# Scores from keys that are carried through the folded matrix, eight batches at a time, in place of projected queries

## The reference, cut to what matters

```python
vcq = concatenate([v, where(row_zero, 0, q)], -1)
self_feat = vcq @ W_self.T + b_self
output = self_feat
for d in range(2):
    A = adj if d == 0 else swapaxes(adj, 1, 2)
    A = A[:, :, :20, :]
    cond, vb = A.sum(-1), A @ w_bias + b_bias
    kv = self_feat[:, :20]
    qh, kh = heads(self_feat @ Wq[d].T + bq[d]), heads(kv @ Wk[d].T + bk[d])
    aff = einsum('bnhd,bmhd->bnhm', qh, kh) / sqrt(32)
    w = softmax(where(cond > 0, aff, -9e15) + vb)
    output += einsum('bnhf,hgf->bnhg', einsum('bnhm,bmf->bnhf', w, kv), Wout[d]) + bout[d]
return v + relu(output)
```

## Time and profile before

| what | value |
|---|---|
| median of 3 runs | 1905.44 us |
| the profiled execution's own time | 1906.23 us |
| its span | 1904.4 us |
| TensorE matmul busy | 1887.3 us (99%), 11020 records |
| VectorE busy | 1303.7 us (68%) |
| ScalarE busy | 575.5 us (30%) |
| GpSimd busy | 836.6 us (44%) |
| granted TensorE clock | 0.999 of full |

### The profile page before, as it was taken

The page is one execution under the profiler, slowest core; times in us unless marked ns, Lnnn a source line. Parts: engine busy times, 40 slices in busy tenths (PEclk is TensorE's granted clock), DMA queues, the critical chain, the costliest instruction groups (busy, mean ns, idle before and its releaser), DMA issues.

```text
span 1904.4 us, 34516 instructions
## 1 busy us (share of the span) xinstructions
PE 1887.3 (99%) x11020; PEld 1646.9 (86%) x11020; DVE 1303.7 (68%) x1897; ACT 575.5 (30%) x1189; POOL 836.6 (44%) x746
## 2 busy tenths in 40 slices
PE   8999999999999999999999999999999999999999
PEld 6899999888888888888888888888888888888887
DVE  3433232477777777777777777777777777777776
ACT  3333232233333333333333333333333333333332
POOL 0332222354444444444444444444444444444443
PEclk9999999999999999999999999999999999999999
DMA  7123324544444444444444444444444444444431
GB/s 214 34 84 89 96 90 99 136 113 122 122 122 119 118 120 121 121 121 121 121 121 121 121 121 121 121 121 121 121 121 121 121 121 121 121 121 121 121 100 63
DMA packets 227951, 219.87 MB, mean 115 GB/s; under 512 B 58176, under 2 KB 179008, under 8 KB 223808
## 3 DMA queue, kind: packets, MB, share of 16 engines
q1 hardware_dynamic: 223440, 219.24, 42.6%
q10 hardware_dynamic: 4464, 0.02, 0.1%
HBM read 164.39 MB, written 54.79 MB: 115 GB/s over the span
## 4 chain that ended last, share of the span: by engine, by line
PE 95%; DVE 1%; DMA 0%; issue 0%; SPq 0%; POOL 0%; ACT 0%; ACTq 0%; DVEq 0%
PE bank L1517 37%; PE bank L1463 19%; PE bank L849 14%; PE bank L1451 12%; PE bank L1487 8%; PE bank L1476 4%; PE bank L857 0%; PE bank L1436 0%; DMA adj<-in_mask_BxSxSx_ik 0%; PE bank L1526 0%; DVE nodes_t L88 0%; DVE qt_main L1276 0%; SPq L650 0%; DVE nodes_t L1212 0%; POOL rc L1152 0%
## 5 line engine op out<-in xcount | busy, mean ns | idle before, releaser
L1152 POOL TENSOR_TENSOR rc<-nzb,cqg 128x512 f32<-128x512 bf16 x256 | 265.1, 1041 | 419.9 <-DVE qt_main L1276 409.3
L1451 PEld LDWEIGHTS bank<-kbd,qt_main 128*128 128x128 f32 x2048 | 243.6, 192 | 19.1 <-DVE sc L1240 13.2
L1276 DVE SCALAR_TENSOR_TENSOR qt_main<-bank,bq_all,rc 128x512 f32<-128x512 f32 x256 | 190.2, 743 | 89.0 <-PE bank L1517 89.0
L1118 POOL TENSOR_TENSOR sc<-sc,mx 128x640 f32<-128x640 f32 x128 | 163.3, 1276 | 199.1 <-DVE mx L1245 198.7
L1451 PE MATMUL bank<-kbd,qt_main 128*128 128x80 f32 x2048 | 247.4, 274 | 0.2
L1362 ACT ACTIVATE wtt<-bank 128x384 f32<-128x384 f32 (+1 forms) x256 | 111.1, 435 | 381.7 <-PE bank L1476 381.6
L1251 DVE TENSOR_REDUCE sm<-sc 128x32 f32<-128x640 f32 x128 | 104.6, 817 | 162.7 <-ACT sc L1354 162.7
L1517 PE MATMUL bank<-nodes_h,wq_h 128*128 128x512 f32 x512 | 210.1, 410 | 1.9 <-DVE qt_main L1276 1.9
L1517 PE MATMUL bank<-xh_odd,wq_h 128*128 128x512 f32 x512 | 210.5, 411 | 0.0
L1517 PE MATMUL bank<-xh_odd,wq_l 128*128 128x512 f32 x512 | 202.4, 395 | 0.0
L1517 PE MATMUL bank<-nodes_h,wq_l 128*128 128x512 f32 x512 | 202.1, 395 | 0.0
(11 more groups left out here) (130 smaller groups left out, 3816.8 us busy)
## 6 DMA issues: line engine op xcount, KB each, us to landing
rows<-in_x SPq DMA_DIRECT2D x128, 256.0 KB, 5.0
xk<-in_x SPq DMA_DIRECT2D x32, 1024.0 KB, 6.1
res<-c_dram SPq DMA_DIRECT2D x32, 1024.0 KB, 4.7
out<-res SPq DMA_DIRECT2D x128, 256.0 KB, 2.1
adj<-in_mask_BxSxSx_ik SPq DMA_DIRECT2D x32, 440.0 KB, 5.6
adj<-in_mask_BxSxSx_ik SPq DMA_DIRECT2D x128, 110.0 KB
k_dram<-kv_kst SPq DMA_DIRECT2D x64, 160.0 KB, 1.8
v_dram<-kv_vt SPq DMA_DIRECT2D x256, 40.0 KB
```

The source lines that it names most:

```text
L1118: pool.tensor_tensor(s, s, mx[:, b % 2, :].unsqueeze(2).to_broadcast([P, DIRS * H, NG]), ALU.subtract).then_inc(s_shifted, 1)
L1152: pool.tensor_tensor(rc[:, c % 2, :].rearrange("p (b n) -> p b n", b=G), nzb[:, par, :].rearrange("p (b n) -> p b n", b=G), cqg[:, par, c, ...
L1276: nc.vector.scalar_tensor_tensor(out=qt[:, c, :], in0=bank[c % 2][:], scalar=bq_all[:, c:c + 1], in1=rc[:, c % 2, :], op0=ALU.add, op1=ALU ...
L1451: mm = nc.tensor.matmul(dst, qt[:, c, b * N:b * N + N], kbd[:, c, :, b * NG:b * NG + NG], start=True, stop=True)
```

## The change

The scores of node n and key m of head h are x_n A k_m plus terms of the condition and the biases, with A the folded matrix and k_m only 32 numbers long. The changed kernel multiplies A with the keys first. `main_loop` is replaced by `window_loop`, in 64 slots of one pair of batches each, with ramps of a few slots at both ends; the hardware loop takes four slots an iteration. A unit is one direction and half of the heads. In each slot, one unit of keys of a **window of eight batches** (160 columns a chunk of four heads) is carried through the folded matrix, and the scores of that unit are taken for the four pairs of the window ("ages" 3 to 0); after four slots a pair has all its scores.

- `fold_high` and `fold_low` store the folded matrix unsplit in fp32, by rows (`a_rows`).
- `generate` (steps 0 to 4) multiplies with contraction 32: strip r (partitions 32r to 32r+31, one head) goes to PSUM bank r. Step 0 has 41 output rows (`zl`: condition columns of the eight batches and the query bias), steps 1 to 4 have 128. 40 plain fp32 products of 160 columns a window.
- ScalarE evicts every strip's bank by an instruction of its own (`constants_high`, `keys_out`), VectorE makes the low part of step 0 (`constants_low`, L1250), and TensorE waits strip by strip (`z_low`, `gen_taken`).
- `scores` now has, for each of eight batch units, four plain fp32 products of 160 columns with contraction 128 and one fp32r product of `flags` and `zc` with contraction 41.
- GpSimd adds x at the end (`finish`), after a clip on ScalarE (`clip`). The sums of x's rows are taken from a load of x of their own (`xs`).
- Self features, transposes, values, edge lists and softmax keep their arithmetic, in pairs in place of groups of four.

```diff
-            nc.vector.tensor_tensor(wq_l[:, m // C, m % C, :], bank[6 + m % 2][:],
-                                    wq_h[:, m // C, m % C, :].bitcast(F32), ALU.subtract).then_inc(fold_l, 1)
+            nc.vector.tensor_copy(a_rows[:, m, 2:C, :],
+                                  bank[6 + m % 2][:].rearrange("q (p j) -> q j p", j=C)[:, 2:C, :]).then_inc(fold_l, 1)
...
+        def generate(t, step):
+            d, hh = unit(t)
+            lo, hi = window(t)
+            if step == 0:
+                pe.wait_ge(key_loaded[t.par], 16 * (t.half + 1))
+                pe.wait_ge(zl_ready, 2 * (t.n + 1) if t.real() else 2 * PAIRS)
+            for c in range(2):
+                o = C * d + 2 * hh + c
+                for r in range(NQ):
+                    if c == 0 and step == 1:
+                        pe.wait_ge(z_low, NQ * t.n + r + 1)
+                    elif c == 0 and (step > 1 or due(t.n)):
+                        pe.wait_ge(gen_taken, NQ * (C * t.n + max(step - 2, -1)) + r + 1)
+                    s = slice(Q * r, Q * r + Q)
+                    rhs = key_tile[s, t.par, c, lo * NG:hi * NG]
+                    dst = slice(c * UN + lo * NG, c * UN + hi * NG)
+                    if step == 0:
+                        mm = nc.tensor.matmul(low_banks[0:ZR, r, dst], zl[s, o, :], rhs, start=True, stop=True)
+                    else:
+                        mm = nc.tensor.matmul(low_banks[:, r, dst], a_rows[s, o, step - 1, :], rhs, start=True, stop=True)
+            mm.then_inc(pe_gen, 1)
...
-            for c in range(NC):
-                d, o = c // C, c % C
-                dst = (S0, S1)[d][:, o * HC * NG:(o + 1) * HC * NG]
-                mm = nc.tensor.matmul(dst, qt[:, c, b * N:b * N + N],
-                                      kbd[:, c, :, b * NG:b * NG + NG], start=True, stop=True)
+            for b in range(2):
+                w = 2 * (AGES - 1 - a) + b
+                dst = s_bank(t, a)[:, b * UN:b * UN + UN].rearrange("p (c r m) -> p c r m", c=2, r=NQ)
+                for j in range(C):
+                    if opening and b == 0 and j == C - 1:
+                        pe.wait_ge(gen_taken, NQ * (C * t.n + C))
+                    mm = nc.tensor.matmul(dst, xt[:, j, p.ring + b, :], kx[:, t.par, j, :, :, w, :].rearrange("p r c m -> p c r m"), start=(j == 0), stop=False)
+                mm = nc.tensor.matmul(dst, flags[0:ZR, p.ring + b, :], zc[0:ZR, t.par, :, :, w, :].rearrange("p r c m -> p c r m"), start=False, stop=True)
             mm.then_inc(pe_s, 1)
...
+        def constants_low(t):
+            dve.wait_ge(z_high, NQ * (t.n + 1))
+            lo, hi = window(t)
+            o, i = taken(zc[Q:ZR, t.par], lo, hi), generated(Q, ZR, lo, hi)
+            for r in range(NQ):
+                nc.vector.tensor_tensor(o[:, r], i[:, r], o[:, r].bitcast(F32), ALU.subtract).then_inc(z_low, 1)
...
+        def keys_out(t, j):
+            act.wait_ge(pe_gen, STEPS * t.n + 2 + j)
+            lo, hi = window(t)
+            o, i = taken(kx[:, t.par, j], lo, hi), generated(0, P, lo, hi)
+            for r in range(NQ):
+                nc.scalar.activation(o[:, r], i[:, r], ACT.Copy).then_inc(gen_taken, 1)
...
+            if soft.real():
+                scores(t, 3)
+            if has_window(nxt):
+                generate(nxt, 0)
...
+                turn_weights(late, 1, 0)
+            if t.back(2).real():
+                scores(t, 2)
+            if late.real():
+                turn_weights(late, 1, 1)
+            if has_window(nxt):
+                generate(nxt, 1)
+            if late.real():
+                values(late, 1)
+            if t.back(1).real():
+                scores(t, 1)
+            if has_window(nxt):
+                generate(nxt, 2)
+            if soft.real():
+                self_features(soft, 0, range(0, 2))
+                turn_weights(soft, 0, 0)
+                self_features(soft, 0, range(2, C))
+                turn_weights(soft, 0, 1)
+            if has_window(nxt):
+                generate(nxt, 3)
+            if t.real():
+                scores(t, 0)
...
+            if soft.real():
+                values(soft, 0)
+            if has_window(nxt):
+                generate(nxt, 4)
+            if soft.real():
+                self_features(soft, 1, range(0, C))
```

More of the change, by code:

```diff
@@ L1000, in main_loop, with __init__, back, real @@
     wtt_ready = sem("wtt_ready")
+    c_scaled = sem("c_scaled")
     pe_self = sem("pe_self")
     pe_out = sem("pe_out")
+    out_taken = sem("out_taken")
+    clipped = sem("clipped")
     res_ready = sem("res_ready")
-    S0, S1 = bank[2], bank[3]
-    def turn_bank(part, last):
-        return bank[0] if last and part == 1 else bank[7]
+    OUT, TURN = bank[6], bank[7]
+    class Pair:
+        def __init__(self, k, c):
+            self.k, self.c = k, c
+            self.n = 4 * k + c
+            self.half = 2 * k + c // 2
+            self.par = c % 2
+            self.ring = 2 * (c % AGES)
+        def back(self, a):
+            return Pair(self.k, self.c - a)
+        def real(self):
+            return not isinstance(self.k, int) or 0 <= self.n < PAIRS
+    def ages(t):
+        return [a for a in range(AGES - 1, -1, -1) if t.back(a).real()]
+    def scored(t, a):
+        if isinstance(t.k, int):
+            earlier = sum(len(ages(Pair(0, u))) for u in range(t.n))
+            return earlier + len([o for o in ages(t) if o >= a])
+        return 4 * t.n - 2 - a
+    def has_window(t):
+        return not isinstance(t.k, int) or 0 <= t.n < PAIRS + AGES - 1
+    def window(t):
+        ws = [2 * (AGES - 1 - a) for a in ages(t)]
+        return min(ws), max(ws) + 2
+    def generated(first, last, lo, hi):
+        return low_banks[first:last, :, 0:2 * UN].rearrange("p r (c x) -> p r c x", c=2)[:, :, :, lo * NG:hi * NG]
+    def taken(home, lo, hi):
+        return home.rearrange("p r c w m -> p r c (w m)")[:, :, :, lo * NG:hi * NG]
+    def unit(t):
+        u = t.c % 4
+        return u // 2, u % 2
+    def edge_group(t):
+        return (t.n + 2) // 2 if isinstance(t.k, int) else 2 * t.k + (t.c + 2) // 2
+    def has_edges(g):
+        return not isinstance(g, int) or 0 <= g < EG
+    def slots(eng, body, first):
+        for n in range(first, 4):
+            body(Pair(n // 4, n % 4))
+        with eng.Fori(1, PAIRS // 4 - 1) as k:
+            for c in range(4):
+                body(Pair(k, c))
+        for n in range(PAIRS - 4, PAIRS + 4):
+            body(Pair(n // 4, n % 4))
     def value_pieces():
@@ L1581, in tensor_program, with flag_rows, turn_mask @@
-        groups(pe, group)
-    return sync_program, vector_program, gpsimd_program, scalar_program, tensor_program
+        def flag_rows(p):
+            pe.wait_ge(nz_ready, 3 * p.n + 3)
+            for b in range(2):
+                mm = nc.tensor.matmul(TURN[0:ZR, b * N:b * N + N], nzm[:, p.ring + b, :], identity_b[:],
+                                      start=True, stop=True)
+            mm.then_inc(pe_e, 1)
+        def turn_mask(g):
+            pe.wait_ge(m_done[1], g + 1)
+            nc.tensor.transpose(TURN[:, 0:EDGE * NG], m1r[:], identity[0:EDGE * NG, 0:EDGE * NG]).then_inc(pe_m1, 1)
@@ L1586 @@
+        slots(pe, slot, -2)
+    return ((sync_program, vector_program, gpsimd_program, scalar_program, tensor_program),
+            early_loads, early_turn)
 _INS = ["x", "cond_1024", "mask_BxSxSx11_ik0", "L0_cond_W_self", "L0_cond_b_self", "L0_cond_w_bias",
```

1034 lines of the change are left out of this document (504 added, 530 removed).

## The result

The changed kernel takes **2182.76 us** (median of 4 runs, 2181.78 to 2186.63) against 1905.33 in the runs of the kernel before beside it: ratio 1.1461, 95% interval 1.1441 to 1.1481. The forecast was 2162, so the number was off by 21 us of 277. Its steps were not right, though: two terms of opposite sign cancelled. The profiled execution took 2181.9 us with a span of 2180.1.

What follows compares the result with a forecast made beforehand. TensorE's issue time was taken as the bound: 361.1 + 20 + 64 x 18.58 + 67 windows of generation at 8.2 + 19 + 8 + 14, with 1.8 around the span, gave 2162 us; range 1860 to 2440.

Steps and rivals of the forecast that it cites:

- What bounds the kernel: Kernel before: TensorE's issue time sets the time, 47.96 of 47.97 us per group of four batches; other engines stay hidden.
- Term 2: New scores on TensorE: 8 units x 4 products x 2 records x 0.134 = 8.60 us, flags matmuls 0.89, per slot.
- Term 4: Generation of carried keys: 80 records a window, 8.2 us if weight loads queue; bounds 2.7 to 10.7.
- g: TensorE time to generate the carried keys of one window, forecast at 8.2 us; break-even with the kernel before at 4.37.
- rival A: Generation strips run four at a time: g 2.7, slot 21.3 us plus 1.4 us of waits, 1880 us; chance 0.23.
- Term 5: Changes between array shapes on TensorE, 28 a slot: bounds nothing to 0.28 us each, nothing taken in the forecast.
- rival C: Array shape changes, 28 a slot at 0.14 us: 251 us more (2413 or 2226 in all), upper bound 500; chance 0.21.
- The trace has no matmul on a part of the array: Generation products of contraction 32: the earlier trace shows no such matmul, so their price was only bounded, 2.7 to 10.7 us.
- Waits, 0.3 us a slot: TensorE waits inside a slot, at key banks in step 1 and the second transpose of soft weights: 19 us in all.
- Ends: Outside the steady loop: 20 us before the first window's step 1, 8 for thin slots, 14 for the last pair.

## Why the prediction came out, and what was wrong in it

- **What bounds the kernel** (TensorE's issue time): right, though TensorE is busy for 94% of the span and not 99%. ScalarE took 61.23 / 4 = 15.3 us a slot (forecast 17.4), VectorE 15.5 (16), GpSimd 10.0 (10); all stayed hidden but for one take-out.
- **Term 2, records of 160 columns at 0.134 us**: right as a price for a run of equal records: 1.16 for a unit forecast at 1.18 once the shape stays the same.
- **Term 4, g = 8.2, "a queue of loads is the one behaviour of narrow products that the trace does show"**: this step failed. The loads of the earlier trace rows all fill the whole array; they say nothing of loads into four separate strips, which ran side by side. Measured g is 3.77, 4.43 less a slot, 297 us over 67 windows. Of the 3.77 the streams of four strips side by side are 80 x 0.134 / 4 = 2.7, rival A's g; the other 1.1 are the edges inside the five steps. The wrong step was to take the nearest row where its mechanism did not carry over. The Trainium skill, "TensorE: Matmul & The Clock Gate", Part 3, has four row tiles 3.07 times as fast at 512 columns, by which g would be 3.5, an estimate. The run on one strip against the change gives 3.1, so it agrees; the strips' starts lie 6 to 7 ns apart here, where that page has some 4.
- **Term 5, "I take nothing in the forecast"**: this step failed in the other direction. A change of shape costs 0.18 to 0.2 us, between the middle (0.14) and the upper bound (0.28) of rival C. The count was off too: the trace has 25 changes a slot and not 28, since three flags products lead straight into another shape. 25 x 0.19 = 4.8 us a slot, and as much is found: 2.67 in scores and flags, 1.1 inside the generation steps, 0.93 in self features, values, transposes and flag rows. The last were not measured by a run of their own, but the starts show them: of the 20 records of the values, 17 take 0.112 us and the three beside a change 0.205, 0.214 and 0.213, which is the whole 0.30; a self feature behind a generation takes 0.333 against 0.233. The Trainium skill, "TensorEngine Tiling (Array Packing)", Key Properties, says that changing the tiling mode drains TensorE; the gaps agree, and they put a price on it.
- **"The trace has no matmul on a part of the array"**: it has one, L1526 with contraction 80, and it stands among its neighbours without any gap:
```profile
914.80 0.40 PE L1517 MATMUL bank<-xh_odd,wq_l 128*128 128x512 f32 x1
915.04 0.23 PE L1526 MATMUL bank<-identity,m1r 80*128 80x80 f32 x1
915.07 0.48 PE L1463 MATMUL bank<-ws_h,xh_odd 128*128 128x512 f32 x1
915.39 0.40 PE L1463 MATMUL bank<-ws_l,xh_odd 128*128 128x512 f32 x1
```
It starts 0.24 us behind a record of 512 columns, and 0.32 + 0.03 us lie between it and the second self feature, as behind the narrow products of the earlier trace rows. So this row would have supported "nothing", and would have misled: 80 rows next to 128 cost nothing, 41 or 32 rows cost 0.19 us.
- **Waits, 0.3 us a slot**: wrong in place and size. I looked at key evictions (2.5 us in all, right to be small) and not at the take-out, 50.4 / 64 = 0.8 a slot, nor at the end of a pass, 29.6 / 56 = 0.5. The latter had no row before, since the kernel before has no such wait.
- **Ends**: 13 loop ends stand 110.6 us apart on average (568.50 to 1895.75, twelve passes), 27.65 a slot with the low clock. 361.1 + 64 x 27.65 leaves 49 us of the span for the ends, where 20 + 8 + 14 and three windows of g came to 67. Step 1 of the first window did wait for VectorE, as foreseen, now 8.23 us behind edge lists and low parts, and in the stretch from 361 to 460 TensorE stood idle for 24 us, with the clock at 0.79.

So 27.08 a slot was forecast and 27.65 came, out of -4.4 (strips), +3.6 (the other work of TensorE), +1.0 (idle) and +0.4 (clock). The rivals were each one mechanism: A had the strips right and its slot at 22.7, C had a price of shapes (at 0.14 too low) on top of a wrong g. Their combination was the truth and had no chance of its own: A's 1880 and C's 251 give 2131, with no better knowledge than the prediction had. That the forecast of 2162 came near is luck: the strips were put 4.4 us too dear and the rest 5 us too cheap, and nothing in the prediction ties the one to the other.

The 2 us at a loop end are, by the traces, a wait for instructions. When TensorE was slower (all strips on one) they were 5.4 us in all instead of 29.6, and with the take-out first 42.1, as if its instructions came at a fixed time and TensorE got there sooner or later. The transfers show that time. Shortly before each of the thirteen products behind an end, the changed kernel's trace has one transfer of 16 KB on the queue of instructions, q8, and the product starts 2.61 to 2.71 us after that transfer does, whether TensorE waited 1.3 or 3.2 us; with all strips on one it is 2.6 to 2.95 us, with the take-out first 2.6 to 3.1. Between 600 and 1900 us the kernel before has 4 transfers on this queue and no such wait, the changed kernel 106, and the one written out 83, with no jump and no such wait. What stays open is which size of the loop's body brings this on (a pass has 834 product records here and 2 x 274 in the kernel before): no run changed it.

## What to carry to other kernels

Products on parts of the array really do share it, but each switch between these shapes costs about a fifth of a microsecond: a product with few rows in the middle of full ones is cheaper padded with zeros to their shape (118 us here for two memsets and a slice). When two unknowns are independent, give their combination a line among the cases; a forecast that lands because two errors cancel has been luck. Count the switches in the order in which the products are issued, too. A saving of one wait is given to the next one in line, so read the list of waits after each edit, and judge edits together.

## What was not expected of the hardware

- Idle TensorE of 2.8 us was followed, about 1.3 us after its return, by some 7 us at the lower clock, although it was full by then. In the change the same followed idles of 2.83, 2.34 and 2.78 us at length, others between 2.09 and 3.24 in part, and did not follow 2.04, 1.93, 1.66 and 1.29, nor one of 2.43.
- The pass of a loop of four slots costs TensorE 1.3 to 3.2 us of idle time at its end; its next product starts 2.6 to 2.7 us after an instruction transfer does, however long it waited.
- A change between contraction 128 and 41 or 32 costs TensorE 0.18 to 0.2 us, one between 128 and 80 nothing.
- Four strips of plain fp32 products overlap fully, their weight loads too, and their order within a step of eight is worth 0.02 us (one run).
- A moving operand in pieces of 20 elements is as fast as one in a row.
